# A four-layer transformer-like kernel on one core: every piece moved to a newly found place, six filler matmuls left out

## The chip, the cores and the metric

One Trainium2 chip, one NeuronCore, one launch. The time is device microseconds of one execution. The kernel before takes 2603.42 us, the median of three runs (2602.71 to 2609.87).

## The reference, cut to what matters

32 batches (`B`), 256 tokens, 256 features, 16 heads of 16. Four layers follow each other for every batch; batches don't touch.

```python
# L0: layer norm over the whole (S, D) of a batch, FiLM and a gate from t, W_in; the same again, W_out; residual
# L1: token layer norm with scale and shift from a timestep; attention with a 16x256x256 bias and a mask; FF (256 -> 1024 -> 256)
x = x + (ctx @ Wo + bo)
x = x + _gelu2(_ln(x) * g2 + beta2 @ W1 + b1) @ W2 + b2
# L2: stencil: gradients and second differences over (S, D), times dt, max(., 0)
# L3: causal attention, then FF with the exact gelu; gate against the input
return x + g * (x2 - x)
```

## The kernel before, in words

The kernel is one program for five engines with no loop on the chip: `build` writes out each engine's instructions in order. TensorE (PE) does matmuls and the turns (transposes by the identity), VectorE (DVE) the additions, the score-plus-bias reductions and half of the evacuations of turned scores, ScalarE (ACT) the exponentials, gelus and the other half, GpSimd (POOL) mask additions, reciprocal roots and several elementwise steps, and SyncE (SP) issues every DMA. A semaphore wait stands ahead of each piece that needs one; an engine never passes a piece that waits.

**What sets the order.** Time is counted in ticks. Batch b of layer 1 begins at tick 64 b and of layer 3 at 64 b + 160 (`begin`); its eight units (pairs of heads, called `_1[b.n]` and `_3[b.n]`) are four ticks apart. Each piece has a place, in ticks from that begin: in `P` for the middle batches, in `OWN` for batches 0, 1 and the last two (-2, -1), in `SPLIT` for units of layer 3. `place` looks it up. Each engine runs through all ticks, and within a tick through its pieces in the fixed order of its function. So a place says only where a piece stands in its engine's own order, nothing of when it runs.

**Pieces that the prediction names**, in the order of the work: `n1_stats`, `n1_sum`, `n1_center` (L969), `n1_scale` (L974, L978), `n1_gate` (L982), `win`, then the same with `n2_` (`n2_ones` is a matmul with ones between statistics and sum), `wout`, `x1` (L1077 and the token statistics), `x1_rstd` on POOL, `x1_norm` on ACT, `ada` (L603, L605) on POOL, `t1` (turn, L1514), `q1`, `k1`, `v1`. A unit is `stack` (nine DMAs), `score0/1` (L1538), `bias0/1` (L1010), `exp0/1` (L1249), `flip0/1` (L1548), `ev0` (L1254) and `ev1` (L1017), `pv` (L1563), `cx`, `ct`, `pvn`. Behind attention come `c1`, `o1`, `m1`, `t2`, `t2_out`, `t2_lo`, `w1` (four steps, L1447), `w1_out` (L1275), `w1_gelu`, `w2` (L1525), `f1`, the stencil `s_...` (`s_re` is L1122 and L1126), `m3`, `t3` and the same in layer 3: `c3` (turn), `c3_out`, `o3`, `m4`, `m4_norm`, `t4` (turn), `t4_out` (L1373), `t4_lo` (L949), `w3` (L1447), `w3_out`, `w3_gelu`, `w4` (L1525), `out`. `xb` (L595), `y3`, `q3_lo`, `k3_lo`, `mask_add` are POOL's. In the set-up, `film`, `adas` (L747), `split_p1` with `_hi` (`first_gains`, L834 to L854; `first_spread` on PE, L1470) and `_lo` (L860) make conditioning rows and scaled half-precision weights; `t1_lo` is L1085.

In each step of `w1` and `w3` the next step writes the one bank that ACT's `w1_out` or `w3_out` must first have read. Only for the last batch do two banks alternate.

**Fillers.** `warm` issues matmuls of the identity whose result nobody reads; `keep` does so behind a named piece of a named batch, by the table `WARM`, and waits for VectorE's last `pvn` first. One filler shows as two instructions (L1397) in the profile.

`Lane.wait_ge` drops a wait whose value its engine has already waited for.

Of the kernel before, what the change touches and what calls it, by code (L numbers as in the profile page):

```python
# [49 lines left out]
def begin(layer, b):  # L50
# [6 lines left out]
    "score0": -1, "score1": -1, "bias0": 0, "bias1": 0, "exp0": 1, "exp1": 2, "flip0": 8, "flip1": 8, "ev0": 7,  # L57
    "ev1": 9, "pv": 14, "cx": 13, "ct": 17, "pvn": 17, "ld_bt": -12, "mask_add": -23, "stack": -8, "ld_x": -78,
    "ld_xn": -37, "ld_ab": -36, "ld_mask": -117, "mask": -34, "n1_stats": -75, "n1_ones": -69, "n1_sum": -69,
# [6 lines left out]
    "f1": 74, "s_pm": 63, "s_b": 67, "s_r": 75, "s_rp": 82, "s_re": 96, "s_ha": 81, "s_w": 97, "s_ab": 97,  # L66
    "s_row": 98, "s_mm": 103, "s_f": 103, "ld_w1": -24, "ld_sten": -46, "ld_w3": -277, "coefs": -21,
# [6 lines left out]
    "out": 74, "st_out": 71,  # L74
# [32 lines left out]
        "y3": 60, "m4_rstd": 249, "m4_b": 298, "ld_x": -76, "ld_xn": -71, "ld_ab": -70, "ld_mask": -17,  # L107
        "ld_bt_1": -13, "stack_1": -12, "s_row": 96, "stack_3": -39, "st_out": 840,
    },
# [7 lines left out]
        "t2_lo": 70, "f1": 89, "s_r": 94, "s_rp": 94, "s_re": 94, "s_ab": 99, "s_f": 104, "m3": -54, "t3_lo": -37,  # L117
# [7 lines left out]
        "m4_b": 656, "ld_x": -88, "ld_xn": -61, "ld_ab": -39, "ld_mask": -139, "ld_bt_1": -22, "stack_1": -17,  # L125
        "stack_3": 217, "st_out": 980,
    },
# [71 lines left out]
def build(nc, A, OUT, scr, NB=32):  # L199
# [21 lines left out]
    with ExitStack() as ctx:  # L221
# [427 lines left out]
        def vector():  # L649
# [382 lines left out]
            def front(t):  # L1032
# [6 lines left out]
                for b in at(t, "n1_center"):  # L1039
                    V.wait_ge(p_wout, b)  # L1040
                    all_center(XT, sm1, v_n1)
# [798 lines left out]
```

## Time and profile before

| what | value |
|---|---|
| time, median of three runs | 2603.42 us |
| the profiled execution, first to last instruction | 2603.7 us |
| busy: PE, PE weight load, DVE, ACT, POOL | 2470.5, 2005.6, 2043.6, 2115.3, 1536.1 us |
| instructions | 57961 |
| DMA | 287.67 MB, 110 GB/s on average |

An engine's busy time is the union of its instructions' time. A matmul's end is modelled and overlaps the next one's start, so a busy PE isn't a PE at its peak. The weight-load row (PEld) is TensorE too: it loads the next matmul's weights while one runs, and an idle stretch of more than some 0.1 us there, with a named releaser, is where TensorE waited for data. Idle time of an engine that nobody waits for costs nothing. The granted clock is a share of TensorE's full clock.

### The profile page before, as it was taken

Reading aid. Unit: us, or ns where it says so; the run is one execution under the profiler, and the core shown is the slowest. Engines: PE = TensorE matmul, PEld = TensorE weight load, DVE = VectorE, ACT = ScalarE, POOL = GpSimd, SP = SyncE. Lnnn points to the kernel's source line nnn. Section 1 sums busy time; section 2 is a strip of 40 time slices with the busy share of each in tenths; the row PEclk is TensorE's granted clock in tenths of the full one; section 3 lists DMA queues with packets and bytes.
Section 4 is the critical chain, followed back from the end, with each engine's and each line's share of the span. In section 5 each row is a group of like instructions: output and inputs, shape, how many; then the busy total and the mean of one; then the engine's idle time right before and its main releaser. Section 6 shows DMA issues by size and latency. Waiting matters only on the chain.

```text
span 2603.7 us, 57961 instructions
## 1 busy us (share of the span) xinstructions
PE 2470.5 (95%) x19148; PEld 2005.6 (77%) x19148; DVE 2043.6 (78%) x7387; ACT 2115.3 (81%) x4694; POOL 1536.1 (59%) x1487
## 2 busy tenths in 40 slices
PE   6878999999999999999999999999999999999987
PEld 5666778778877877887887788778878877877776
DVE  6787878788888778888787888878888888878653
ACT  2466888888898888889888888988888888888875
POOL 2566666556666656666665656666556576655421
PEclk6899999999999999999999999999999999999999
DMA  5433443333344333334443333444433344433211
GB/s 205 120 119 105 121 127 113 111 106 106 107 122 126 112 110 108 107 105 122 126 115 108 108 107 106 122 127 115 114 110 100 105 121 125 123 105 96 75 29 33
DMA packets 178537, 287.67 MB, mean 110 GB/s; under 512 B 46080, under 2 KB 99328, under 8 KB 177984
## 3 DMA queue, kind: packets, MB, share of 16 engines
q1 hardware_dynamic: 178240, 283.97, 38.5%
q8 instruction: 155, 2.54, 0.4%
q14 instruction: 142, 1.16, 0.2%
HBM read 174.64 MB, written 8.45 MB: 70 GB/s over the span
## 4 chain that ended last, share of the span: by engine, by line
PE 69%; DVE 15%; SPq 4%; ACT 4%; issue 3%; POOL 2%; DMA 2%; DVEq 0%; POOLq 0%; ACTq 0%
PE bank L1525 17%; PE bank L1447 12%; PE bank L1548 10%; PE bank L1538 6%; PE bank L1563 6%; PE bank L1507 6%; DVE PB L1010 4%; PE bank L1514 3%; SPq L496 3%; PE bank L1459 3%; PE bank L1701 2%; DVE bank L969 2%; PE bank L1436 2%; SPq L492 1%; DMA Ks<-KU 1%
## 5 line engine op out<-in xcount | busy, mean ns | idle before, releaser
L1249 ACT ACTIVATE PB<-PB,mx 128x256 f32<-128x256 f32 (+1 forms) x2048 | 831.4, 473 | 35.7 <-DVE mx L1010 34.7
L579 POOL TENSOR_TENSOR BT<-BT,MN 128x1024 f32<-128x1024 f32 x256 | 556.9, 2180 | 122.5 <-DMA BT<-in_bias 121.0
L1548 PE MATMUL bank<-ident,PB 128*128 128x128 f32 x3584 | 486.4, 274 | 11.5 <-ACT PT L1254 5.5
L1010 DVE CUSTOM_DVE_ANT_0 PB<-bank,BT 128x256 f32<-128x256 f32 x1024 | 372.0, 418 | 137.8 <-PE bank L1538 132.8
L1548 PEld LDWEIGHTS bank<-ident,PB 128*128 128x128 f32 x3584 | 421.6, 141 | 63.4 <-ACT PB L1249 10.6
L1447 PE MATMUL bank<-TN,WS_w 128*128 128x256 f16 x3072 | 378.8, 273 | 38.7 <-ACT BB L1275 19.6
L1538 PE MATMUL bank<-Ks,Qs 96*128 96x512 f32 (+1 forms) x1024 | 364.6, 430 | 25.5 <-DMA Ks<-KU 12.0
L1017 DVE COPY PT<-bank 128x512 f32<-128x512 f32 (+1 forms) x512 | 315.9, 617 | 87.5 <-PE bank L1548 85.8
L1447 PEld LDWEIGHTS bank<-TN,WS_w 128*128 128x128 f16 x3072 | 282.5, 98 | 120.1 <-ACT BB L1275 35.4
L1254 ACT ACTIVATE PT<-bank 128x512 f32<-128x512 f32 (+1 forms) x512 | 272.3, 532 | 94.9 <-PE bank L1548 90.6
L1010 DVE CUSTOM_DVE_ANT_0 PB<-bank,caus 128x128 f32<-128x128 f32 (+1 forms) x1024 | 306.6, 350 | 42.3 <-PE bank L1538 42.2
L1563 PE MATMUL bank<-PT,VW 128*32 128x256 f32 (+1 forms) x4096 | 248.2, 360 | 4.4 <-DVE CX L1027 2.4
L1525 PE MATMUL bank<-Wf,BB 128*128 128x256 f32 x1024 | 236.8, 379 | 0.8 <-ACT BB L1264 0.6
L1525 PE MATMUL bank<-Wf,AA 128*128 128x256 f32 x1024 | 236.0, 383 | 0.5 <-ACT AA L1351 0.4
L1538 PEld LDWEIGHTS bank<-Ks,Qs 96*128 96x128 f32 x1024 | 168.1, 192 | 67.7 <-DVE mx L1010 22.3
L1525 PEld LDWEIGHTS bank<-Wf,AA 128*128 128x128 f32 x1024 | 192.2, 191 | 29.5 <-issue 0.9
L1525 PEld LDWEIGHTS bank<-Wf,BB 128*128 128x128 f32 x1024 | 189.6, 190 | 25.1 <-issue 1.7
L1563 PEld LDWEIGHTS bank<-PT,VW 128*32 128x32 f32 x4096 | 107.5, 109 | 98.7 <-issue 49.0
L554 POOL TENSOR_SCALAR smm<-smm 128x2 f32<-128x2 f32 x32 | 7.2, 226 | 280.0 <-DVE smm L991 280.0
L1010 DVE DVE_READ_ACCUMULATOR2_ANT mx<- 128x1 f32 x2048 | 169.0, 83 | 0.0
L1275 ACT ACTIVATE BB<-bank,cols 128x256 f32<-128x256 f32 x256 | 107.4, 470 | 44.3 <-PE bank L1447 44.3
L1260 ACT ACTIVATE ET<-bank 128x256 f32<-128x256 f32 x256 | 97.2, 380 | 46.8 <-PE bank L1563 42.7
(285 smaller groups left out, 4735.9 us busy)
## 6 DMA issues: line engine op xcount, KB each, us to landing
BT<-in_bias SPq DMA_DIRECT2D x256, 512.0 KB, 4.3
Qs<-QH SPq DMA_DIRECT2D x512, 64.0 KB, 2.4
Ks<-KH SPq DMA_DIRECT2D x1024, 32.0 KB, 2.0
Qs<-QU SPq DMA_DIRECT2D x256, 64.0 KB, 2.4
Ks<-KU SPq DMA_DIRECT2D x512, 32.0 KB, 2.0
XT<-in_xT SPq DMA_DIRECT2D x32, 256.0 KB, 2.8
X<-in_x SPq DMA_DIRECT2D x32, 256.0 KB, 2.9
AB<-ada_rows SPq DMA_DIRECT2D x32, 256.0 KB, 3.7
```

The costliest lines, as they stand in the source:

```text
L579: G.op.tensor_tensor(v2(BT[k % 4]), v2(BT[k % 4]), MN[:, :].unsqueeze(1).broadcast_to([128, 2, 512]), ALU.add).then_inc(g_bt, 1)
L1010: V.op.tensor_tensor_reduce(PB[(2 * D + q) % 6][:, h * 256:h * 256 + w], bS[q][:, h * w:h * w + w], plus, -1.0, 3.0e38, ALU.add, ALU.min, ...
L1017: V.op.tensor_copy(flipped(u.D, 1)[:, 0:w], bP[1][:, 0:w]).then_inc(v_ev, 1)
L1249: S.op.activation(o, o, ACT.Exp, scale=-1.0, bias=mx[u.layer][:, c:c + 1]).then_inc(a_exp, 1)
L1254: S.op.activation(flipped(u.D, 0)[:, 0:w], bP[0][:, 0:w], ACT.Copy).then_inc(a_ev, 1)
L1275: S.op.activation(half(out, m), half(ps, m), ACT.Identity, scale=scale(m), bias=bias(m)).then_inc(sem, 1)
L1447: last = T.op.matmul(half(ps, m), w, v[:, k * 256:k * 256 + 256], start=(k == 0 and i == 0), stop=(k == 1 and i == 2))
L1507: last = T.op.matmul(half(ps, m), x[:, k * 256 + m * 128:k * 256 + m * 128 + 128], Wf[:, a + k * 256:a + k * 256 + 256], start=(k == 0), s ...
L1525: last = T.op.matmul(half(ps, q), x[:, f * 256 + q * 128:f * 256 + q * 128 + 128], Wf[:, c:c + 256], start=(g == 0 and f == 0 and q == 0), ...
L1538: T.op.matmul(bS[q][:, 0:2 * w].rearrange("p (h k) -> p h k", h=2), Qs[i][0:96, et * 256 + q * 128:et * 256 + q * 128 + 128], k2[:, :, 0:w ...
L1548: last = T.op.transpose(bP[h][:, c * 128:c * 128 + 128], PB[(2 * u.D + q) % 6][:, h * 256 + k * 128:h * 256 + k * 128 + 128], ident[:, :])
L1563: last = T.op.matmul(half(bV, J % 2)[32 * s:32 * s + 32, q:256], VW[x][:, v:v + 32], flipped(u.D - 1 + et, h)[:, k * 256:k * 256 + 256 - q ...
```

## The change

All places of `P`, `OWN` and `SPLIT` are replaced by others, found by a search that replays the engines in order. No piece's instructions change. Six fillers go: one behind `n2_ones` of batch 2, four behind `n1_ones` of batch 3, one behind `v1` of batch 3. Two waits each are written ahead of `n1_center` and `n2_center`. The diff, cut to its core (the places of which the text speaks; the full tables change by a few ticks throughout):

```diff
 P = {
-    "cx": 13, "n1_stats": -75, "n1_sum": -69, "n1_gate": -53, "n2_center": -33, "x1": -29, "x1_norm": -27,
-    "n1_ones": -69, "v1_out": -7, "s_re": 96, "s_f": 103, "w2": 68, "m1": 49, "m1_rstd": 30, "m1_b": 56,
-    "t4": 58, "t4_out": 56, "y3": -8, "q3_lo": -37, "k3_lo": -33, "stack": -8, "st_out": 71,
+    "cx": 14, "n1_stats": -70, "n1_sum": -67, "n1_gate": -48, "n2_center": -36, "x1": -28, "x1_norm": -25,
+    "n1_ones": -68, "v1_out": -10, "s_re": 97, "s_f": 104, "w2": 69, "m1": 50, "m1_rstd": 24, "m1_b": 32,
+    "t4": 56, "t4_out": 55, "y3": -15, "q3_lo": -23, "k3_lo": -32, "stack": -6, "st_out": 83,
...
 WARM = {
-    "start": 24, "c1": 12, "n1_ones_0": 2, "v1": 9, "win_1": 5, "w1_0": 3, "n2_ones_2": 1, "n1_ones_3": 4,
-    "v1_3": 1, "v3": 10,
+    "start": 24, "c1": 12, "n1_ones_0": 2, "v1": 9, "win_1": 5, "w1_0": 3, "v3": 10,
 }
...
                 for b in at(t, "n1_center"):
                     V.wait_ge(p_wout, b)
+                    V.wait_ge(p_n1, b + 1)
+                    V.wait_ge(v_n1, 10 * b + 4)
                     all_center(XT, sm1, v_n1)
...
                 for b in at(t, "n2_center"):
                     V.wait_ge(p_win, b + 1)
+                    V.wait_ge(p_n2, b + 1)
+                    V.wait_ge(v_n2, 10 * b + 4)
                     all_center(FY, sm2, v_n2)
```

What this does to the engines' orders in a middle period of 64 ticks (brackets: batch, with +0 the one whose layer 1 begins there; all that isn't named keeps its order):

```text
PE    was: w2.2[-1], score[.2], w2.3[-1], flip[.0]       now: score[.2], w2.2[-1], flip[.0], w2.3[-1]
PE    was: flip_1[.4], pv_1[.3], t4[-3]                  now: flip_1[.4], t4[-3], pv_1[.3]
PE    was: score_3[-2.7], n1_ones[+2], w1.1, flip_3      now: score_3[-2.7], w1.1, flip_3, n1_ones[+2]
ACT   was: exp1_1[.5], m4_norm, ev0_1[.4], win_out, t4_out   now: m4_norm, exp1_1[.5], ev0_1[.4], t4_out, win_out
ACT   was: exp1_1[.7], w3_out.1                          now: w3_out.1, exp1_1[.7]
ACT   was: x1_norm, exp0_3[-2.1], exp1_3[-2.1]           now: exp0_3[-2.1], exp1_3[-2.1], x1_norm
DVE   was: n1_gate, s_r, bias_1[.3], v3_out, bias_1[.4]  now: s_r, bias_1[.3], v3_out, bias_1[.4], n1_gate
DVE   was: n2_sum, ev1_1[.5], pvn_1[.3], n2_center       now: n2_sum, n2_center, ev1_1[.5], pvn_1[.3]
DVE   was: bias0_3[-2.0], s_re, bias1_3[-2.0], ev1, n2_gate   now: bias0_3, bias1_3, ev1, n2_gate, s_re
DVE   was: x1, bias0_3[-2.1], bias1_3[-2.1]              now: bias0_3[-2.1], bias1_3[-2.1], x1
DVE   was: s_f, bias0_3[-2.2], bias1_3[-2.2]             now: bias0_3[-2.2], bias1_3[-2.2], s_f
POOL  was: q3_lo, k3_lo, mask_add[.6]                    now: mask_add[.6], k3_lo, mask_add[.7], m4_rstd, q3_lo
SP    was: st_out, stack_3[-2.6], ld_x, ld_bt[+1.0]      now: stack_3[-2.6], ld_bt[+1.0], st_out, ld_bt[+1.1], ld_x
```

In the set-up (batch 0) `split_p1_hi` moves on DVE from ahead of `n2_center` to behind `n2_gate` (on PE it stays ahead of `wout`), `x1` from behind `split_p1_lo` to ahead of it, and `adas` from behind `n1_gate` to ahead of it; on PE `win[1]` and `n2_ones[1]` come ahead of the first scores. At the end `w3` of batch 30 is spread between the scores of batch 31, and the last step of `w4[30]` moves from behind `t4[31]` to ahead of it.

## Rows read from the trace of the kernel before

**Rows 1.** The page, part 1: busy us (share of the span), instructions

```profile
PE 2470.5 (95%) x19148; PEld 2005.6 (77%) x19148; DVE 2043.6 (78%) x7387; ACT 2115.3 (81%) x4694; POOL 1536.1 (59%) x1487
```

**Rows 2.** Three stretches: PE, PEld, DVE, ACT, POOL busy, granted clock, DMA share, GB/s

```profile
0.00:300.00 300.00, 239.72 (x1588) 189.40 (x1589) 226.66 (x737) 162.89 (x346) 160.61 (x150) 0.86 0.45 139
300.00:2300.00 2000.00, 1962.76 (x15485) 1601.74 (x15484) 1631.07 (x5938) 1730.19 (x3851) 1252.38 (x1213) 1.00 0.40 112
2300.00:2604.00 304.00, 268.02 (x2079) 214.48 (x2077) 185.87 (x714) 222.18 (x498) 123.16 (x126) 0.99 0.26 69
```

**Rows 3.** The chain of waits, in order of time: start us, us, what

```profile
1193.77 5.29 PE bank L1525 x24
...
1269.21 5.29 PE bank L1525 x24
```

**Rows 4.** Waits of the weight loads, 1421 to 2025 us: us in total, times, longest

```profile
PEld bank L1447 <- ACT BB L1275: 8.7, 16, 0.7
...
PEld bank L1447 <- DVE TN L949: 4.3, 16, 0.3
...
PEld bank L1538 <- DVE mx L1010: 2.2, 8, 0.3
```

**Rows 5.** Timeline of the weight loads, one quiet period [idle before <-releaser]

```profile
1208.49 0.42 PEld L1514 LDWEIGHTS bank<-ident,CX 128*128 128x128 f32 x4 [0.17 <-issue]
...
1219.70 1.21 PEld L1447 LDWEIGHTS bank<-TN,WS_w 128*128 128x128 f16 x12 [0.31 <-DVE TN L949]
...
1228.77 0.19 PEld L1538 LDWEIGHTS bank<-Ks,Qs 96*128 96x128 f32 x1 [0.28 <-DVE mx L1010]
```

**Rows 6.** Timeline of ACT, the same period

```profile
1217.29 0.82 ACT L1275 ACTIVATE XT<-bank,cols 128x256 f32<-128x256 f32 x2
1218.33 0.60 ACT L1373 ACTIVATE TN<-bank 128x512 f16<-128x512 f32 x1 [0.22 <-PE bank L1514]
```

**Rows 7.** Timeline of DVE, the same period

```profile
1218.96 0.69 DVE L949 TENSOR_TENSOR TN<-bank,TN 128x512 f16<-128x512 f32 x1 [0.73 <-ACT TN L1373]
...
1223.49 1.77 DVE L969 SCALAR_TENSOR_TENSOR bank<-XT,sm,gT 128x512 f32<-128x512 f32 x1
...
1227.48 0.35 DVE L1122 TENSOR_TENSOR sme<-X,er 128x8 f32<-128x8 f32 x2
...
1227.95 0.41 DVE L1010 CUSTOM_DVE_ANT_0 PB<-bank,caus 128x256 f32<-128x256 f32 x1
...
1232.30 0.67 DVE L1077 TENSOR_TENSOR X<-bank,X 128x512 f32<-128x512 f32 x1
```

**Rows 8.** Timeline of POOL, the same period

```profile
1223.41 1.29 POOL L595 TENSOR_TENSOR X<-X,rows 128x512 f32<-128x512 f32 x1
...
1238.43 1.27 POOL L605 TENSOR_TENSOR X<-X,AB 128x512 f32<-128x512 f32 x1
```

**Rows 9.** Timeline of PE, the same period

```profile
1241.66 0.60 PE L1514 MATMUL bank<-ident,X 128*128 128x128 f32 x4
```

**Rows 10.** Timeline of PE, 100 to 420 us: fillers (L1397)

```profile
169.45 0.49 PE L1397 MATMUL bank<-ones,ident 128*128 128x128 f32 x2 [1.38 <-DVE CX L1027]
...
202.64 1.14 PE L1397 MATMUL bank<-ones,ident 128*128 128x128 f32 x8
```

**Rows 11.** One stretch behind the fillers, columns as rows 2

```profile
230.00:250.00 20.00, 15.84 (x102) 10.87 (x101) 19.61 (x69) 9.03 (x22) 11.32 (x13) 0.83 0.29 72
```

**Rows 12.** Timeline of DVE, set-up of batch 0

```profile
29.88 0.67 DVE L747 TENSOR_TENSOR PB<-bank,PB 32x512 f32<-32x512 f32 x1
...
36.01 0.27 DVE L834 TENSOR_REDUCE ap<-bank 4x1 f32<-4x128 f32 x1
...
39.45 0.75 DVE L969 SCALAR_TENSOR_TENSOR bank<-XT,sm,gT 128x512 f32<-128x512 f32 x1
...
56.42 0.75 DVE L1085 SCALAR_TENSOR_TENSOR H<-bank,wp,H 128x512 f16<-128x512 f32 x1 [3.12 <-ACT H L1330]
```

**Rows 13.** Timeline of PE, the last 30 us

```profile
2586.02 1.89 PE L1525 MATMUL bank<-Wf,BB 128*128 128x256 f32 x8
```

More of the change, by code:

```diff
@@ L56 @@
 P = {
-    "score0": -1, "score1": -1, "bias0": 0, "bias1": 0, "exp0": 1, "exp1": 2, "flip0": 8, "flip1": 8, "ev0": 7,
-    "ev1": 9, "pv": 14, "cx": 13, "ct": 17, "pvn": 17, "ld_bt": -12, "mask_add": -23, "stack": -8, "ld_x": -78,
-    "ld_xn": -37, "ld_ab": -36, "ld_mask": -117, "mask": -34, "n1_stats": -75, "n1_ones": -69, "n1_sum": -69,
[6 rows of a table removed]
-    "f1": 74, "s_pm": 63, "s_b": 67, "s_r": 75, "s_rp": 82, "s_re": 96, "s_ha": 81, "s_w": 97, "s_ab": 97,
-    "s_row": 98, "s_mm": 103, "s_f": 103, "ld_w1": -24, "ld_sten": -46, "ld_w3": -277, "coefs": -21,
+    "score0": -1, "score1": -1, "bias0": 0, "bias1": 0, "exp0": 2, "exp1": 3, "flip0": 8, "flip1": 8, "ev0": 7,
+    "ev1": 9, "pv": 14, "cx": 14, "ct": 17, "pvn": 17, "ld_bt": -13, "mask_add": -26, "stack": -6, "ld_x": -71,
+    "ld_xn": -41, "ld_ab": -37, "ld_mask": -85, "mask": -31, "n1_stats": -70, "n1_ones": -68, "n1_sum": -67,
[6 rows of a table added]
+    "f1": 73, "s_pm": 59, "s_b": 60, "s_r": 74, "s_rp": 81, "s_re": 97, "s_ha": 74, "s_w": 98, "s_ab": 98,
+    "s_row": 101, "s_mm": 103, "s_f": 104, "ld_w1": -24, "ld_sten": -46, "ld_w3": -277, "coefs": -21,
     "split_p1": -55, "split_p1_hi": -50, "split_p1_lo": -45, "split_w1": -8, "split_w1_hi": -4, "split_w1_lo": -2,
     "split_p3": 46, "split_p3_hi": 50, "split_p3_lo": 54, "split_w3": 82, "split_w3_hi": 88, "split_w3_lo": 92,
[4 rows of a table removed]
-    "out": 74, "st_out": 71,
[4 rows of a table added]
+    "st_out": 83,
 }
@@ L91 @@
     -2: {
[15 rows of a table removed]
-        "y3": 60, "m4_rstd": 249, "m4_b": 298, "ld_x": -76, "ld_xn": -71, "ld_ab": -70, "ld_mask": -17,
-        "ld_bt_1": -13, "stack_1": -12, "s_row": 96, "stack_3": -39, "st_out": 840,
[6 rows of a table added]
+        "m1": 50, "t2_lo": 60, "f1": 80, "s_r": 82, "s_rp": 90, "s_re": 91, "s_ab": 99, "s_f": 112, "m3": -46,
[9 rows of a table added]
     },
     -1: {
[6 rows of a table removed]
-        "t2_lo": 70, "f1": 89, "s_r": 94, "s_rp": 94, "s_re": 94, "s_ab": 99, "s_f": 104, "m3": -54, "t3_lo": -37,
[7 rows of a table removed]
-        "m4_b": 656, "ld_x": -88, "ld_xn": -61, "ld_ab": -39, "ld_mask": -139, "ld_bt_1": -22, "stack_1": -17,
-        "stack_3": 217, "st_out": 980,
-    },
[10 rows of a table removed]
-        "s_rp": 86, "s_re": 97, "s_w": 99, "s_ab": 102, "s_f": 109, "t3_lo": -44, "bias1_3": 0, "v3_out": 15,
[8 rows of a table removed]
-        "s_row": 93, "stack_3": -10, "st_out": 84,
-    },
[7 rows of a table removed]
-        "t2_lo": 62, "f1": 84, "s_r": 85, "s_rp": 92, "s_re": 92, "s_w": 98, "s_ab": 98, "s_f": 102, "m3": -38,
[7 rows of a table removed]
-        "ld_mask": -32, "ld_ab": -21, "ld_bt_1": 0, "stack_1": 4, "s_row": 100, "stack_3": -8, "st_out": 75,
[6 rows of a table added]
+        "t2_lo": 70, "f1": 86, "s_r": 90, "s_rp": 93, "s_re": 97, "s_ab": 98, "s_f": 101, "m3": -54, "t3_lo": -39,
[7 rows of a table added]
+        "m4_b": 734, "ld_x": -100, "ld_xn": -68, "ld_ab": -27, "ld_mask": -100, "ld_bt_1": -14, "stack_1": -12,
+        "stack_3": 273, "st_out": 1017,
+    },
[17 rows of a table added]
+        "y3": -33, "m4_rstd": 33, "m4_b": 55, "scr": -390, "ld_mask": -325, "ld_sten": -150, "ld_ab": -181,
+        "ld_w1": -71, "ld_w3": -93, "ld_bt_1": 0, "stack_1": 0, "s_row": 103, "stack_3": -13, "st_out": 89,
+    },
[7 rows of a table added]
+        "t2_lo": 63, "f1": 80, "s_r": 80, "s_rp": 85, "s_re": 94, "s_w": 97, "s_ab": 97, "s_f": 101, "m3": -50,
[7 rows of a table added]
+        "ld_mask": -31, "ld_ab": -41, "ld_bt_1": -8, "stack_1": -1, "s_row": 91, "stack_3": -13, "st_out": 75,
     },
@@ L168 @@
 SPLIT = {
-    "bias1_3": 1, "exp0_3": 2, "exp1_3": 3, "ev0_3": 8, "ev1_3": 10, "pv_3": 13, "cx_3": 12, "ct_3": 16,
-    "pvn_3": 18, "stack_3": -9,
+    "bias1_3": 0, "exp0_3": 2, "exp1_3": 3, "ev0_3": 8, "ev1_3": 10, "pv_3": 13, "cx_3": 13, "ct_3": 17, "pvn_3": 18,
+    "stack_3": -7,
 }
```

135 rows, old and new, of tables (OWN, P) are left out of this document.

## The prediction, made before the changed kernel was built or run

> **What bounds the kernel now.** I read the page's busy times first: TensorE is busy for 95% of the span, the next engine for 81% [rows 1]. Then the stretches: TensorE's idle time is 60 us in the first 300 us, 37 us in the 2000 us of the middle and 36 us in the last 304 us [rows 2], and its granted clock is full from 300 us on. So the middle is a TensorE stream that another order can't make shorter than its own issue time, and what is to be gained there are short waits that recur in each batch.
>
> The chain of waits gives the period: the same block of 24 matmuls comes at 1193.77 and at 1269.21 us, 75.44 us apart [rows 3]. 28 such periods lie between some 200 and 2300 us; the rest is filling and draining. A busy matmul row hides small waits behind its modelled end, so I go to the weight loads, where they show as idle time with a releaser. Over eight periods (1421 to 2025 us) the largest is L1447 waiting for ScalarE's L1275, 8.7 us for layer 3 alone, 1.09 us a period [rows 4]: the steps of `w3` share one bank with `w3_out`. Smaller are L1447 waiting for VectorE's L949 (`t2_lo`, `t4_lo`), 4.3 us, and L1538 waiting for L1010 (a score that waits for the reductions of the unit before), 2.2 us in 8 times, so once in every period [rows 4]. Places of the kind last named in the table of orders are what the change can mend.
>
> **The change part by part.**
>
> *The added waits* cost nothing. `n1_sum` and `n2_sum` stand ahead of their `center` in both orders and have waited for the same values, so `Lane.wait_ge` issues no instruction. Instructions are the same but for 12 (six fillers), DMAs the same and in number and size.
>
> *`t4` and `t4_out` earlier.* Now `t4_out` starts at 1218.33 behind `win_out` of 0.82 us [rows 6], `t4_lo` at 1218.96 after 0.73 us of idle VectorE [rows 7], and the first `w3` step's weights at 1219.70 after 0.31 us idle, released by it [rows 5]. With `m4_norm` ahead of two exponentials, `t4` ahead of `pv` (some 1 us) and `t4_out` ahead of `win_out`, that input comes at least 0.6 us earlier, and the wait of 0.31 us goes whole. Between 0 and 0.31; I take 0.31. What is late next is the bank's hand-over between the steps of `w3`, whose filling work on PE is the same as before: that 1.09 us stays.
>
> *`s_re` behind `bias1_3[-2.0]`.* From 1227.48 to 1227.95 VectorE does the two edge products and sums between two reductions [rows 7]; the score behind waits 0.28 us for the second reduction [rows 5]. Moved behind, the reduction ends 0.47 us sooner and the wait is gone: 0.28. `s_re` itself feeds the DMA `s_row`, for which `s_mm` has not to wait here; that cover is the three `w4` and score blocks ahead of it.
>
> *`n1_gate` behind `v3_out`.* An elementwise step of 0.67 to 0.69 us [rows 7] leaves the way of `v3_out`, for which `c3` waits (its wait names no releaser, the two are 0.2 us apart): 0.17 [rows 5]. `n1_gate` feeds `win`, two units later on PE; nobody is behind it.
>
> *Given back.* `x1` goes behind four reductions (0.3 to 0.4 us each, 1.4 together, by the one of 0.41 [rows 7]). It starts the longest side chain: `x1` at 1232.30 [rows 7], roots, `x1_norm`, the last `ada` step at 1238.43 for 1.27 us [rows 8], the turn `t1` at 1241.66 [rows 9]. Between the end of `ada` (1239.70) and `t1` there are 1.96 us. Of these 1.4 go, and 0.76 because TensorE comes earlier: 0.2 short; with ScalarE's `x1_norm` also behind four exponentials I take 0.3 us, between 0 and 1.68 (the whole of a further 1.48 us of exponentials, less nothing). `w3_out.1` ahead of `exp1`, `n1_ones` behind two turns, `v1_out` and `ev1` earlier, the spacing of `w2`: each moves a piece into or out of a stretch of at most 0.2 us; together 0, between -0.2 and +0.2. On POOL `q3_lo`, `k3_lo` both go behind `mask_add[.6]`, which no longer waits for ScalarE; `stack_3[-2.0]` needs them 10 ticks later: 0. On SP the stacks are held by their buffers, the same two scores ahead as before, so the new places of `st_out` and `ld_mask` change nothing: 0. `m1_b` now stands ahead of masks and waits for `m1_norm`; behind it on POOL are `m3_rstd` and the mask additions of the next batch, four units early: 0.
>
> So a period gives 0.31 + 0.28 + 0.17 - 0.30 = 0.46 us, 28 periods 12.9 us.
>
> *Fillers.* Eight filler instructions take 0.89 us start to start (202.64 to the next block at 203.53; the row's 1.14 has the modelled end) [rows 10], so twelve take 1.3 us. The filler of batch 2 also waited 1.38 us for a `pvn` [rows 10]. Both lie where TensorE idles anyway, so between 0 and 2.7 us; I take 1.5.
>
> *Set-up.* `first_gains` runs on VectorE from 36.01 to 39.45, right ahead of `n2_center` [rows 12]; moved behind `n2_gate` it gives that chain 3.4 us, and takes back some 1 us as `first_spread` on PE stays ahead of `wout`. `adas` ahead of `n1_gate` can't begin before TensorE's rows are there, at 29.88 [rows 12], and holds the gate for 1.5 us. Net 0.9 us by `x1`. But `split_p1_lo` then follows `x1`: some 4 us of VectorE work in front of `t1_lo`, which had 3.12 us of idle time ahead of it [rows 12]. So nothing is left of it at batch 0. The front of batch 1 (`win`, `n2_ones` ahead of the first scores) gets earlier by a few us, into a stretch where TensorE idles 20%. I take 1.0 us for all, between -3 and +6.
>
> *End.* The `w3` steps of batch 30 between scores of batch 31 fill waits of about 1 us each, some 2.5 us; the last `w4` step ahead of `t4[31]` puts up to 1.89 - 0.4 us in the way of the last chain [rows 13]. I take 1.0, between -2 and +4.
>
> Sum: 12.9 + 1.5 + 1.0 + 1.0 = 16.4 us off the profiled execution's 2603.7, which is 2587.3. That execution stands 0.3 us above the median of the runs, so 2587.
>
> **A rule against the trace.** `n2_center` takes 1.77 us [rows 7] where the same instruction takes 0.75 us in the set-up [rows 12]; POOL's `xb` runs from 1223.41 to 1224.70 [rows 8] beside the long one, and nothing on POOL beside the short. The change puts `n2_center` ahead of `ev1` and `pvn`, so ahead of `xb`, which waits for `n2_rstd` in POOL's order. Then 1.0 us leaves a stretch in which VectorE has no idle time from 1218.96 to 1228.6. This is the rival "larger" below. The Trainium skill ("SBUF — State Buffer", "Summary: rules for kernel authors") says that a VectorE instruction with two SBUF inputs and a GpSimd instruction that reads SBUF block each other, the second waiting for the first to end. By that rule the trace agrees: 1.77 is 0.75 plus 1.02 us.
>
> **The rivals.**
>
> *Larger:* the stretch of VectorE leads TensorE, and the 1.0 us comes on top of 0.46. At most the rest of what weight loads lose there: 28 x 1.0 would be 28; I count half, 14 us: 2573. Against: the named waits for VectorE in the middle are 0.31 + 0.28 us only.
>
> *Given back:* the period is set by the hand-over of the banks and by stacks that land just in time, and the waits mended come back one block later. 0.1 us a period, 2.8, with 3.5 for the rest: 2597.
>
> *Slower:* the chain from `x1` to `t1` comes late. 1.4 us on VectorE and 1.48 us on ScalarE, less the 1.96 of slack, are 0.92 us; `t1` then opens 0.92 us later than now in each period and drags all with it: 25.8 us, less 3.5: 2626. It decides from a delay of 1.96 us on; at 2.3 us the kernel is slower by over 0.3%. For: two engines put the chain behind others. Against: the exponentials can run before `x1_norm`'s roots are ready.
>
> *Clock:* without the fillers the granted clock falls once more. Behind them a stretch of 20 us already has 0.83 [rows 11], which is an alternation of 1.2 and 2.4 GHz; 20 us at 0.83 lose 3.4 us, where TensorE waits anyway. That gives 2590. The Trainium skill ("TensorE: Matmul & The Clock Gate", "Why this matters for your kernels") says that an idle gap drops the clock by half; by it twelve short instructions between others decide nothing, and no run here shows it yet.
>
> *No difference by design:* the waits that are written and not issued are the part of the change that does nothing; a search whose replay misjudges waits could as well end at 2603. It is in "given back".
>
> **How the numbers follow.** Forecast (2579 to 2595) 0.46, clock 0.04 beside it; larger 0.14; given back (2595 to 2609) 0.26; slower 0.10. 0.3% is 7.8 us, about what a measurement of this kernel can tell from no change: faster lies below 2595.6, slower above 2611.2. Faster 0.46 + 0.03 + 0.14 = 0.63, slower 0.10, same 0.27. The range leaves out the slower rival and the far side of the larger one: 2571 to 2608; the forecast's own is 2579 to 2595.
>
> **What would show it.** Right: a period near 75.0 us; no L949 wait ahead of the first `w3` step; no L1010 wait at the score behind `w3.3`; `c3` without its 0.17; L969 of `n2` near 0.8 us. The slower rival: L1514 `<-X` waits for POOL L605 in each period. Given back: same period, other releasers. Wrong altogether: if the gain lies in the first 300 or the last 300 us, or if stacks' DMAs show as the new wait of L1538.

## The result, and the profile after

The changed kernel takes 2638.13 us, the median of four runs (2636.57 to 2643.31), against 2603.07 us of the kernel before on the same chip: a ratio of 1.0134, 95% interval 1.0116 to 1.0151. It is slower by 35 us, and I had forecast 16 us faster. The profiled execution takes 2637.3 us. Times below come from several sessions, in which the kernel before had medians of 2603.1 to 2608.6 us, so runs are compared by their ratio to it.

The page's busy times after answer to [rows 1]. The stretches, in the columns of [rows 2], stand behind them.

```profile
PE 2468.8 (94%) x19136; PEld 2005.4 (76%) x19136; DVE 1991.6 (76%) x7387; ACT 2110.4 (80%) x4694; POOL 1539.3 (58%) x1487
```

```profile
0.00:300.00 300.00, 232.27 (x1500) 181.48 (x1501) 205.34 (x712) 156.97 (x332) 155.10 (x144) 0.85 0.43 135
300.00:2300.00 2000.00, 1938.66 (x15391) 1585.60 (x15389) 1586.68 (x5890) 1710.38 (x3819) 1251.71 (x1205) 1.00 0.40 112
2300.00:2640.00 340.00, 297.91 (x2250) 238.35 (x2248) 199.54 (x788) 243.06 (x544) 132.51 (x140) 0.96 0.25 66
```

TensorE's work is the same and its idle time in the middle has grown from 37 to 61 us, at a full clock. VectorE is busy 52 us less: its instructions are the same, so some of them got shorter, and TensorE got nothing of it.

The place of the loss shows when the same piece is compared in both traces. The first matmul of `win` of each batch starts, against the kernel before, in the profiled executions:

| kernel | batch 2 | batch 4 | batch 29 | end | a period, batches 4 to 29 |
|---|---|---|---|---|---|
| before | 160.41 us | 302.62 us | 2197.91 us | 2603.7 us | 75.81 us |
| changed | -0.2 | +8.5 | +24.0 | +33.6 | 76.43 us |

So 8.5 us are lost while the pipeline fills, 15.5 us over 25 middle periods (0.62 each, where I had forecast a gain of 0.46) and 9.6 us behind batch 29.

Each row is one execution, and the ends scatter from one execution to the next. The kernel before, run 10 and run 11 below have the same instructions in the same order up to `win` of batch 2, and it starts at 160.4, 154.1 and 157.7 us; runs 2 and 12 are the same up to `win` of batch 4, and it starts at 310.8 and 314.2 us. So a difference of under some 6 us at batch 2, or 3 us at batch 4, shows nothing by itself.

The waits of the middle answer to [rows 4]. From the waits of the changed kernel, 1421 to 2025 us (engine, line, releaser: us in total, times, longest):

```profile
PEld bank L1539 <- DMA Ks<-KU: 11.1, 15, 1.3
PEld bank L1448 <- ACT BB L1276: 9.7, 16, 0.8
...
PE bank L1539 <- DMA Ks<-KU: 7.3, 13, 1.1
...
PEld bank L1539 <- issue: 6.6, 16, 0.4
...
PEld bank L1448 <- DVE TN L946: 1.9, 8, 0.2
```

The two waits that I wanted mended are: the one for TN went from 4.3 us in 16 times to 1.9 in 8 (only layer 1's is left), the one for `mx` in 8 times is off the list. In their place scores wait for the stacks, 15 times in eight periods, so twice in each. The same in the whole kernel, first a row of the page of before and then two of the changed kernel's page (busy us, mean ns, idle before and its releaser):

```profile
L1538 PE MATMUL bank<-Ks,Qs 96*128 96x512 f32 (+1 forms) x1024 | 364.6, 430 | 25.5 <-DMA Ks<-KU 12.0
```

```profile
L1539 PE MATMUL bank<-Ks,Qs 96*128 96x512 f32 (+1 forms) x1024 | 362.5, 431 | 60.9 <-DMA Ks<-KU 53.3
...
L1539 PEld LDWEIGHTS bank<-Ks,Qs 96*128 96x128 f32 x1024 | 167.9, 193 | 119.3 <-DMA Ks<-KU 70.3
```

What is behind such a wait stands in the chain of waits of the changed kernel (start us, us, what):

```profile
1421.67 0.64 ACT KH L1293
1422.38 0.96 POOL KU L564
1423.63 1.28 POOL QU L561
1424.93 0.57 SPq L489
...
1430.05 2.40 DMA Ks<-KU
1432.49 0.73 PE bank L1539 x2
...
1459.29 0.72 POOL smt L554
1460.28 1.25 POOL QU L561
1461.54 0.56 SPq L489
...
1467.41 2.01 DMA Ks<-KU
1469.46 0.62 PE bank L1539 x2
```

Two chains in one period, both through POOL and SP. In the first, `k1_lo` (KU) waits for ScalarE's `k1_out`, `q1_lo` (QU) runs behind it, and only then can SP issue the nine DMAs of `stack_1[+1.0]`, the first three of which carry Q. In the second, `q3_lo` stands in POOL's order behind `mask_add[.7]` and `m4_rstd` (smt); `stack_3[-2.0]` begins at 1461.54 us, where `q3_lo` has just ended (1460.28 + 1.25). POOL's order in a middle period has changed by more than the table of orders says. The two places that matter, in both kernels:

```text
was: m1_rstd, q1_lo, k1_lo, mask_add[.0], m3_rstd            now: m1_rstd, k1_lo, q1_lo, m1_b, mask, m3_rstd, mask_add[.0]
was: mask_add[.4], q3_lo, mask_add[.5], s_pm, k3_lo,         now: mask_add[.4], mask_add[.5], s_pm, s_b, mask_add[.6],
     mask_add[.6], s_b, mask_add[.7], m4_rstd                     k3_lo, mask_add[.7], m4_rstd, q3_lo
```

The same stretch in POOL's and SP's timelines, and the row of POOL's waits over eight periods:

```profile
1456.39 2.14 POOL L576 TENSOR_TENSOR BT<-BT,MN 128x1024 f32<-128x1024 f32 x1
1458.71 0.23 POOL L551 TENSOR_SCALAR smt<-smt 128x2 f32<-128x2 f32 x1 [0.18 <-DVE smt L988]
...
1460.23 1.29 POOL L561 TENSOR_TENSOR QU<-QU,QH 128x512 fp32r<-128x512 f32 x1
```

```profile
1457.22 0.58 SPq L465 DMA_DIRECT2D X<-in_x  x1
1461.54 0.56 SPq L489 DMA_DIRECT2D Qs<-QH  x1
```

```profile
POOL smt L551 <- DVE smt L988: 5.1, 8, 0.9
```

SP is free at 1457.80 us, and the last score that reads the stack's buffer has started at 1456.97; SP then stands still for 3.7 us until `q3_lo` is done. `m4_rstd` waits for VectorE's statistics, but only 0.18 us here and 0.2 to 0.9 us in the eight periods. The rest is POOL's own work: the end of the mask addition (0.7 us), the four steps of `m4_rstd` (1.6) and `q3_lo` itself (1.3). The kernel before has `q3_lo` long before it is wanted. Its POOL, SP and PE timelines, in the period of [rows 5]:

```profile
1199.20 1.28 POOL L564 TENSOR_TENSOR QU<-QU,QH 128x512 fp32r<-128x512 f32 x1 [0.27 <-ACT QH L1292]
...
1214.47 0.71 POOL L557 TENSOR_TENSOR smt<-smt,mh 128x2 f32<-128x2 f32 x1
```

```profile
1213.26 0.56 SPq L492 DMA_DIRECT2D Qs<-QH  x1
1213.86 0.59 SPq L492 DMA_DIRECT2D Qs<-QU  x1
1214.49 0.59 SPq L492 DMA_DIRECT2D Qs<-QH  x1
1215.12 2.57 SPq L496 DMA_DIRECT2D Ks<-KH  x4
1217.73 1.23 SPq L496 DMA_DIRECT2D Ks<-KU  x2
```

```profile
1223.37 0.60 PE L1538 MATMUL bank<-Ks,Qs 96*128 96x256 f32 x2
```

`q3_lo` is done 12.8 us before the first DMA of `stack_3[-2.0]`, the stack's nine DMAs keep SP for 5.7 us, and its first score starts at 1223.37 us, 10.1 us behind the stack's start and without waiting for it. In the changed kernel the stack starts 7.9 us before its first score, which waits for it. The stack is late by what `q3_lo` is late, and `q3_lo` is late because it stands seven pieces further back. No run puts `q3_lo` between `k3_lo` and `m4_rstd`, so what each of the seven costs isn't shown.

### The profile page after: what moved, and what is told of

The parts are those of the page before. It is cut to its first block, busy times and chain, and to the rows that moved or that the text cites. A ratio compares the mean times of both kernels' runs of the same rounds, so it can differ in the third digit from the quotient of the medians.

```text
span 2637.3 us, 57930 instructions
## 1 busy us (share of the span) xinstructions
PE 2468.8 (94%) x19136; PEld 2005.4 (76%) x19136; DVE 1991.6 (76%) x7387; ACT 2110.4 (80%) x4694; POOL 1539.3 (58%) x1487
## 4 chain that ended last, share of the span: by engine, by line
PE 66%; SPq 12%; POOL 6%; DMA 5%; DVE 5%; ACT 4%; issue 2%; POOLq 0%; DVEq 0%; ACTq 0%
PE bank L1526 17%; PE bank L1448 13%; PE bank L1549 9%; SPq L493 7%; PE bank L1564 6%; PE bank L1508 6%; PE bank L1539 6%; DMA Ks<-KU 4%; SPq L489 4%; POOL QU L561 2%; PE bank L1515 2%; PE bank L1702 2%; PE bank L1460 2%; ACT PB L1250 1%; PE bank L1574 1%
## 5 line engine op out<-in xcount | busy, mean ns | idle before, releaser
L1250 ACT ACTIVATE PB<-PB,mx 128x256 f32<-128x256 f32 (+1 forms) x2048 | 841.2, 474 | 46.7 <-DVE mx L1007 45.7
L1276 ACT ACTIVATE AA<-bank,cols 128x256 f32<-128x256 f32 x256 | 107.4, 471 | 42.6 <-PE bank L1448 42.3
```

What stands on the lines that cost most here:

```text
L1250: S.op.activation(o, o, ACT.Exp, scale=-1.0, bias=mx[u.layer][:, c:c + 1]).then_inc(a_exp, 1)
L1276: S.op.activation(half(out, m), half(ps, m), ACT.Identity, scale=scale(m), bias=bias(m)).then_inc(sem, 1)
```

## The experiments

**Theory A:** POOL's low halves (`q_lo`, `k_lo`) come late in POOL's order, the stacks start late, the scores wait. **Rival B:** the chain from `x1` to `t1` comes late, as in the prediction's slower rival, and the stacks only slip along.

**1. Low halves back, in both layers.**

```diff
 P = {   (the changed kernel's, middle batches)
-    "q1_lo": -33, "k1_lo": -38, "q3_lo": -23, "k3_lo": -32
+    "q1_lo": -27, "k1_lo": -27, "q3_lo": -37, "k3_lo": -33
```

> The changed kernel with q1_lo, k1_lo, q3_lo and k3_lo of the middle batches back where they stood on POOL; every other engine's order is the changed kernel's. Theory A (POOL's low halves come late behind m1_rstd, the mask additions and m4_rstd, the stacks' DMAs behind them, the scores wait for Ks): in 1421 to 2025 us the changed kernel's weight loads at L1539 wait 11.1 us for Ks where the kernel before has 1.2. That 10 us over eight periods is 1.2 us a period, and the period was 0.85 us longer; A expects that wait at 1 to 3 us, a period of 75.0 to 75.6 us and a time of 2612 to 2624 us, since filling and draining, with 17 of the 35 us lost, stay as they are. Rival B (the chain from x1 to t1 comes late, my rival of the prediction, and the stacks wait only because the whole period slipped): the period stays at 76.2 to 76.6 us and the time at 2633 to 2640 us, the wait for Ks turning into a wait of L1515 for X.

Measured: 2819.12 us, ratio 1.0815 (1.0793 to 1.0837). Neither theory: the places, taken from the old table, don't give the old order. `m1_b`, `mask` and `m3_rstd` have moved ahead in the new one, so that `q1_lo` and `k1_lo` came to stand behind all three.

**2. and 3. One layer at a time.** Layer 3 alone (in POOL's order only `q3_lo` moves, back ahead of `s_b`, `mask_add[.6]`, `k3_lo`, `mask_add[.7]` and `m4_rstd`), and layer 1 alone with the unlucky place.

```diff
-    "q3_lo": -23, "k3_lo": -32      (2)
+    "q3_lo": -37, "k3_lo": -33
-    "q1_lo": -33, "k1_lo": -38      (3)
+    "q1_lo": -27, "k1_lo": -27
```

> The changed kernel with only layer 3's q3_lo and k3_lo put back. Theory A expects that the one late stack_3[-2.0] goes and the one late stack_1[+1.0] stays: half of the gain of putting all four back, 7 to 11 us, so 2626 to 2632 us. A variant of A in which only one of the two decides (A3: q3_lo, which goes from 37 to 23 ticks ahead and behind m4_rstd, the longer move): all of the gain, 2612 to 2624 us. Rival B (x1 to t1): 2633 to 2640 us.

> The changed kernel with only layer 1's q1_lo put back ahead of k1_lo. Theory A with equal shares: 2626 to 2632 us. A3 (layer 3 alone decides): 2634 to 2640 us. Rival B: 2633 to 2640 us. If this run gives the whole gain and the one with layer 3 none, the swap of q1_lo and k1_lo, which I had not even costed, is the cause.

Measured: layer 3 alone 2617.88 us, ratio 1.0046 (1.0030 to 1.0061); layer 1 alone 2846.89 us, ratio 1.0924. One instruction of 1.28 us in an earlier place gives back 0.88% of 1.34%, some 23 us: rival B is out as the main cause. In the profiled executions it gives back 17.3 us between batches 4 and 29, 0.69 a period. Run 3 is no test of layer 1, but a price: behind `m1_b`, `mask` and `m3_rstd` instead of ahead of them, the two halves of layer 1 make a period 83.7 us long (mean over batches 4 to 29). From `m1_rstd`'s end at 1460.10 us to `q1_lo`'s start at 1466.24 us run 3 has 1.68 us in which `m1_b` waits for ScalarE and 4.5 us of POOL's own work. That wait, 1421 to 2025 us:

```profile
POOL X L614 <- ACT AA L1270: 11.7, 7, 1.7
```

With layer 3 mended (run 2), the same stretch still shows one late stack in each period:

```profile
PEld bank L1539 <- DMA Ks<-KU: 4.2, 8, 1.2
```

**4. The cause alone.** The kernel before with POOL's new order of the four pieces: `q3_lo` behind `m4_rstd`, `q1_lo` behind `k1_lo`.

```diff
 P = {   (the kernel before)
-    "q1_lo": -27, "k1_lo": -27, "q3_lo": -37, "k3_lo": -33
+    "q1_lo": -26, "k1_lo": -27, "q3_lo": -23, "k3_lo": -32
```

> The kernel before with only POOL's order of q1_lo, k1_lo, q3_lo and k3_lo of the middle batches as in the changed kernel. Theory A: the cause alone, without anything else of the change, makes the kernel before slower by 0.5 to 0.85 us a period over 28 periods: 2617 to 2627 us, and its weight loads at L1538 wait for Ks some 8 to 11 us between 1421 and 2025 us, where they wait 1.2 us now. Rival B: 2600 to 2606 us, no difference. Between them (2607 to 2615): the move costs only together with others that use up the stacks' slack.

Measured: 2638.82 us, ratio 1.0126 (1.0104 to 1.0148). These places alone make the kernel before as slow as the whole change does, but not in the same stretches: from batch 4 to 29 it loses 25.8 us, 1.03 a period, where the change loses 15.5. That the totals agree is chance; that these places bring the wait for Ks and a loss of this size is shown. The waits of the weight loads and of the matmuls, 1421 to 2025 us:

```profile
PEld bank L1538 <- DMA Ks<-KU: 13.5, 16, 2.2
...
PE bank L1538 <- DMA Ks<-KU: 9.4, 14, 2.0
```

**5. Layer 1 put right.** As run 2, with `q1_lo` directly ahead of `k1_lo`.

```diff
-    "q1_lo": -33      (run 2)
+    "q1_lo": -39
```

> The changed kernel with q3_lo and k3_lo of layer 3 back (which alone gave 2618 us) and q1_lo of layer 1 back ahead of k1_lo, where ada's last instruction and m1_rstd stand ahead of both as before. Behind the scores at L1539 the run with layer 3 alone still waits 4.2 us in 8 times for Ks between 1421 and 2025 us, once a period, 0.5 us each. Theory A (every late low half costs): that wait goes, 0.3 to 0.5 us a period over 28 periods, so 2604 to 2610 us. Rival (the swap is covered, only layer 3's halves count): 2615 to 2620 us.

Measured: 2609.67 us, ratio 1.0018 (1.0006 to 1.0030). The swap costs 0.28%, 7 us (0.41%, 11 us, if run 12 is set against run 2), and its wait is gone:

```profile
PEld bank L1539 <- DMA Ks<-KU: 0.8, 3, 0.3
```

From batch 4 to 29 this kernel gains 11.1 us on the kernel before, 0.44 a period, near what the forecast gave for the middle. Run 7, and runs 13 and 15 below, which have this order from batch 4 on, gain 0.41, 0.34 and 0.38. But it comes 15.5 us late to batch 4 and loses 5.4 us behind batch 29.

**6. and 7. Old tables for the ends.** As run 5, with the old tables of the first two and last two batches and all fillers (6), or the old tables of the last two alone (7).

```diff
-OWN = { ... }    (new)
+OWN = { ... }    (of before: 0, 1, -2, -1 in run 6; -2, -1 in run 7)
```

> As the run with all low halves back, and the tables of the first two and the last two batches and the fillers as in the kernel before; the middle batches keep the changed places. Theory A (the rest of the loss is filling and draining, 8 us in batches 2 and 3 and some 9 us behind the last input matmuls): 14 to 18 us less than that run, and 8 to 13 us faster than the kernel before if my three mended waits (0.46 us a period) are worth what I put them at: 2591 to 2597 us. Rival C (given back: the mended waits come back as others): 2601 to 2606 us. If the loss of the first 300 us stays, it comes from the middle places reaching into batches 2 and 3, not from the set-up's tables.

> As the run with all low halves back, and only the tables of the last two batches as in the kernel before. Against the run with all low halves back it gives the price of draining: theory A 7 to 10 us less; a rival, that the end only drags along what came late before, 0 to 3 us less.

Measured: 2664.18 us, ratio 1.0209 (1.0183 to 1.0236), and 2649.18 us, ratio 1.0164 (1.0148 to 1.0181). Both missed: old ends on a new middle are worse than new ends. Run 6 is 22.1 us late at batch 4, run 7 loses 39 us behind batch 29. The tables of the ends fit only the middle that they were found with, so these runs don't give a price of the ends.

**8. The three mended waits alone, on the kernel before.**

```diff
-    "m4_norm": 54, "t4": 58, "t4_out": 56, "win_out": -41, "s_re": 96, "n1_gate": -53
+    "m4_norm": 53, "t4": 56, "t4_out": 55, "win_out": -40, "s_re": 97, "n1_gate": -48
```

> The kernel before with only the three moves for which I forecast the gain: m4_norm, t4 and t4_out earlier, s_re behind bias1_3[-2.0], n1_gate behind v3_out. Without the delayed x1 chain my terms are 0.31 + 0.28 + 0.17 = 0.76 us a period, 21 us over 28: 2582 us if each is worth its wait. Rival C (a mended wait comes back at the next hand-over, since the period is set elsewhere): 2598 to 2606 us. In the trace the wait of L1447 for TN before the first w3 step (4.3 us over eight periods with both layers) and that of L1538 for mx (2.2 us) should be gone in either case.

Measured: 2598.78 us, ratio 0.9976 (0.9965 to 0.9988): 0.24% faster than the kernel before, with run 9 the lowest ratio here. From batch 4 to 29 it gains 10.7 us, 0.43 a period (0.31 and 0.35 in runs 14 and 16 below, which have the same three moves), where the three terms make 0.76. The waits of 1421 to 2025 us show where the rest may have gone:

```profile
PEld bank L1447 <- ACT BB L1275: 9.7, 16, 0.8
PEld bank L1447 <- ACT AA L1275: 7.6, 21, 0.5
PEld bank L1538 <- issue: 6.6, 16, 0.4
...
PEld bank L1447 <- DVE TN L949: 1.6, 7, 0.2
```

TN's wait fell by 2.7 us and that for `mx` (2.2) is gone. But the hand-over of the bank between the `w3` steps rose by 1.0 us against [rows 4], and the score's wait without a releaser from 3.3 us in 8 times (a row of the kernel before) to 6.6 in 16. So 4.3 of the 4.9 us mended came back as other waits. The period gained 3.4 us in eight, more than the difference; wait rows are no full account of a period, and least of all can their sums be taken as a gain.

**9. `n2_center` ahead of `ev1` and `pvn`, on top of run 8.**

```diff
-    "n2_center": -33
+    "n2_center": -36
```

> The kernel before with the three mended waits and also n2_center ahead of ev1_1[.5] and pvn_1[.3], as the change has it. My rival larger: n2_center's 1.7 us fall towards 0.75 because POOL's xb no longer runs beside it, 1 us a period on VectorE, 14 us of the time at half the worth: 2585 us. Its other face, as the periods of 75.07 us with the three mends alone suggest: VectorE isn't what TensorE waits for, L969 gets shorter and the time stays within 3 us of the run with the three mends, 2596 to 2602 us.

Measured: 2602.84 us, ratio 0.9975 (0.9963 to 0.9987), the same as run 8. Durations of that line, `n1_center` and `n2_center` together, 1421 to 2025 us, in the kernel before and in this run (min/median/max ns):

```profile
L969 DVE SCALAR_TENSOR_TENSOR bank<-XT,sm,gT x16: 751/1760/2006, 1450.7 to 2022.2; 128x512 f32<-128x512 f32 x16
```

```profile
L969 DVE SCALAR_TENSOR_TENSOR bank<-XT,sm,gT x16: 748/952/2028, 1446.8 to 2018.1; 128x512 f32<-128x512 f32 x16
```

The eight of `n2_center` alone are the clearer reading: 1.76 to 1.77 us each in the kernel before, 0.75 us each in this run (0.75 in the changed kernel too). So the instruction does get 1.0 us shorter when POOL's `xb` isn't beside it, and the time stays.

**10. `x1` late, alone.**

```diff
-    "x1": -29, "x1_norm": -27
+    "x1": -27, "x1_norm": -25
```

> The kernel before with x1 alone behind four reductions, ev1_1[.7] and pvn_1[.5] (1.1 us of reductions from 1233.90 to 1234.98 us and some 1.3 us for the two others, more than in the change) and x1_norm behind exp0_3[-2.1] and exp1_3[-2.1]. My rival slower: 2.4 us on VectorE are 0.4 us over the slack of 1.96 us, and ScalarE's exponentials can add up to 1.48: the turn t1 comes 0.4 to 1.9 us late in each period, 11 to 53 us more, 2614 us or above, L1514 waiting for X of L605. The other theory, after the period of 75.1 us that the changed kernel reaches once POOL's low halves are back: the chain has more slack than I read, and the time stays at 2602 to 2609 us.

Measured: 2620.00 us, ratio 1.0048 (1.0029 to 1.0067). The forecast of the time was near; its mechanism was not. From batch 4 to 29 the run loses 1.2 us, 0.05 a period, so a delay of some 2.4 us on VectorE (the estimate of its expectation) fits into the slack. At batch 4 it is 7.2 us behind. (At batch 2 it is 6.3 us ahead, but its instructions are still those of the kernel before there, so that is scatter.) Between the two `x1` stands behind `pvn_1[.5]`, and that piece waits for the stencil's DMA through TensorE. From its chain of waits:

```profile
247.41 1.72 DMA AA<-AA
...
249.26 1.97 PE bank L1701 x8
251.23 0.23 PE bank L1573 x2
251.48 0.22 DVE rd L1024
...
251.93 0.69 DVE X L1077
```

The kernel before has `x1` at 247.17 us. In the change `x1` is behind reductions only.

**11. Without the six fillers, alone.**

```diff
-    "w1_0": 3, "n2_ones_2": 1, "n1_ones_3": 4, "v1_3": 1, "v3": 10
+    "w1_0": 3, "v3": 10
```

> The kernel before without the six fillers, nothing else. My term: 0 to 2.7 us less, 1.5 taken: 2602 us. The rival clock: TensorE's granted clock falls more often between 140 and 240 us, 3 to 5 us more: 2607 to 2609 us, with a granted clock below 0.91 in stretches where it is 0.91 to 1.00 now.

Measured: 2605.08 us, ratio 0.9988 (0.9979 to 0.9997), 3 us less. The granted clock looks lower. From the stretches of 20 us of the kernel before and of this run:

```profile
160.00:180.00 20.00, 15.14 (x118) 11.82 (x119) 17.89 (x64) 11.44 (x27) 13.36 (x11) 1.00 0.20 59
180.00:200.00 20.00, 16.25 (x124) 12.12 (x124) 14.53 (x34) 10.36 (x20) 10.19 (x15) 0.91 0.24 78
```

```profile
160.00:180.00 20.00, 14.93 (x103) 11.99 (x96) 17.39 (x61) 10.29 (x25) 11.71 (x12) 0.86 0.09 22
180.00:200.00 20.00, 18.07 (x122) 14.28 (x123) 12.46 (x27) 9.54 (x19) 8.99 (x12) 0.80 0.24 77
```

But it scatters as much with all six fillers there: in the same two stretches run 10 has 0.81 and 0.76, run 8 has 0.91 and 0.83, run 6 has 0.95 and 0.67. So no run shows that the fillers hold the clock.

**12. `q1_lo` back from batch 4 on only.** Run 5, with `q1_lo` of batches 2 and 3 as in the change.

```diff
+    2: {"q1_lo": -33}, 3: {"q1_lo": -33}      (in OWN)
```

> The changed kernel with q3_lo back everywhere and q1_lo back only from batch 4 on (batches 2 and 3 keep it behind k1_lo, as the search found it). The run with both back everywhere lost 7 us more than this order in batches 1 to 3 (15.5 us behind the kernel before at batch 4, where the changed kernel is 8.5 behind) and gained 11 us from there to batch 29. If the place in batches 2 and 3 makes those 7 us: 2601 to 2604 us, no difference from the kernel before, and 8 us behind at batch 4. If they come from q3_lo or from elsewhere: 2608 to 2612 us.

Measured: 2611.41 us, ratio 1.0005 (0.9993 to 1.0018): no difference from the kernel before. Against the kernel before it is 11.5 us behind at batch 4, 0.3 ahead at batch 29 (a gain of 0.47 a period) and 4.8 behind at the end.

**13. `x1` earlier in batches 2 and 3, on top of run 12.**

```diff
+    2: {"x1": -30, "x1_norm": -28}, 3: {"x1": -30, "x1_norm": -28}      (in OWN)
```

> The run with q3_lo back and q1_lo back from batch 4 on (11.5 us behind the kernel before at batch 4), now also with x1 and x1_norm of batches 2 and 3 earlier, ahead of the reductions and exponentials that the change put in front of them. The kernel before with x1 alone late lost 6.5 us at exactly this place and nothing behind it. Theory D (the places in P reach into the filling, where x1 to t1 has no slack): 4 to 7 us of the 11.5 come back, 2601 to 2605 us with the kernel before at about 2605. Rival E (the loss there is made by the late statistics of m1 and by k1_lo ahead of q1_lo, in the chain at 197 to 209 us): 0 to 2 us, 2606 to 2612 us.

Measured: 2613.65 us, ratio 1.0030 (1.0016 to 1.0044), 11.6 us behind at batch 4. The place of `x1` isn't what the filling loses; moved forward it gives nothing back.

**14. Runs 8 and 11 together.**

```diff
-    "m4_norm": 54, "t4": 58, "t4_out": 56, ...      (all of run 8)
+    "m4_norm": 53, "t4": 56, "t4_out": 55, ...
-    "n2_ones_2": 1, "n1_ones_3": 4, "v1_3": 1      (run 11)
```

> The kernel before with the three mended waits and without the six fillers. If the two parts (ratios 0.9976 and 0.9988 alone) add: 0.9964, some 9 us less than the kernel before. If the fillers' gain was chance or the falling clock costs as much as they do: 0.9976, some 6 us less.

Measured: 2604.36 us, ratio 0.9983 (0.9970 to 0.9995). The parts don't add.

**15. and 16. Fillers again.** Run 12 with five of the six back (15), and run 8 with only the one at `n2_ones` dropped (16).

```diff
+    "n1_ones_3": 4, "v1_3": 1      (15, to run 12)
-    "n2_ones_2": 1                 (16, from run 8)
```

> The run with q3_lo back and q1_lo back from batch 4 on, and five of the six fillers back: four behind n1_ones and one behind v1 of batch 3. In both kernels that had the order of before in the filling, taking the fillers out lost some 5 us between the input matmuls of batches 2 and 4, at a granted clock of 0.80 to 0.86 where it had been 0.91 to 1.00. Theory F (the missing fillers make that part of the filling's loss): 3 to 5 us less than the same order without them, so at or just below the kernel before, ratio 0.998 to 0.9995, and the loss at batch 4 falls from 11.5 to 6 to 8 us. Rival G (the fillers do nothing for the time, as in the whole kernel's time with the order of before): ratio 1.000 to 1.003, loss at batch 4 unchanged.

> The kernel before with the three mended waits and only the one filler dropped that waited 1.38 us for a pvn (behind n2_ones of batch 2). Theory F: the five others keep the clock, and the loss of 5 us between batches 2 and 4 of the run without any of the six is gone: ratio 0.9965 to 0.9976 against the kernel before, 6 to 9 us less. Rival G: as without all six, 0.998.

Measured: ratios 1.0001 (0.9988 to 1.0014) and 0.9980 (0.9966 to 0.9994); run 15 is 12.3 us behind at batch 4. Rival G stands: five fillers more or less can't be told apart in the time. Between 180 and 200 us run 15 has them and shows

```profile
180.00:200.00 20.00, 18.46 (x118) 15.09 (x118) 13.71 (x41) 9.29 (x20) 7.35 (x6) 0.74 0.21 70
```

## Why the prediction was wrong

**The step that failed** is one sentence: "On POOL `q3_lo`, `k3_lo` both go behind `mask_add[.6]`, which no longer waits for ScalarE; `stack_3[-2.0]` needs them 10 ticks later: 0." I took a distance in ticks for a time and named no row of POOL (and by the tables the distance of `q3_lo` is 16 ticks, not 10). In ticks `q3_lo` was early enough; on the engine it now stood behind seven more pieces, the last of them `m4_rstd`, and was done 3.7 us after SP had become free for the stack. Put at 0, it measured 0.88% or 23 us (the change against run 2). The swap of `q1_lo` and `k1_lo` stood in neither my list of orders nor my sum and measured 0.28% to 0.41% or 7 to 11 us (run 2 against runs 5 and 12). With `q3_lo` undone everywhere and the swap from batch 4 on the ratio falls from 1.0134 to 1.0005 (run 12), and both on the kernel before make 1.0126 of it (run 4). The sentence that SP's new places change nothing was blind to what SP waits for; no run tries SP's places alone. The prediction did name the sign, the stacks' DMAs as the new wait of L1538, and gave it no chance.

**The sum of the middle** came out near the forecast once POOL was right: 0.34 to 0.47 us a period (runs 5, 7, 12, 13 and 15) for 0.46. That is luck, two errors that cancel. The three mended waits were put at 0.76 and are worth 0.31 to 0.43 (runs 8, 14 and 16); the waits for the hand-over of the bank and at the next score grew meanwhile. That was my rival "given back", true for about half. The delayed chain from `x1` was put at -0.30 and costs 0.05 even where it is delayed by more (run 10).

**Filling** was put at +1.0 and the fillers at +1.5. The change loses 8.5 us by batch 4. The fillers' term is right within its bounds (3 us in run 11, nothing in run 15). A loss is there: the six kernels with the new order in batches 0 to 3 and `q3_lo` right are 8.2 to 15.5 us behind at batch 4 (runs 2, 5, 7, 12, 13, 15), five with the old order are -1.2 to 2.9 us behind (runs 8, 9, 11, 14, 16). What makes it isn't settled: not `x1`'s place (run 13), not the fillers (run 15), and not `q1_lo`'s, for which the place that the search found is no worse there (15.5 and 13.6 us in runs 5 and 7, 11.5 to 12.3 in runs 12, 13 and 15, 8.2 in run 2). In the changed kernel `m3_rstd` of batch 0 gets its statistics on POOL at 196.74 us, 4.5 us later than before (192.21), and `k1_lo`, `q1_lo` and the stack of batch 2 stand behind it (the expectation of run 13 took that piece for `m1`'s). What makes the statistics late I haven't isolated.

**The end** was put at +1.0, and the change loses 9.6 us behind batch 29. That this comes from the new tables of the last two batches isn't shown: with the old tables the same stretch is 2.9 us longer in run 10, 4.1 in run 8, 5.5 in run 9, 8.0 in run 14, 9.4 in run 16 and 11.2 in run 4, and 1.2 us shorter in run 11, always against the one execution of the kernel before. The new order of `w3` and `w4` at the end wasn't tried alone.

**The rivals.** *Larger* is out: `n2_center` got shorter and the time didn't (run 9). The rule of the Trainium skill ("SBUF — State Buffer", "Summary: rules for kernel authors") agrees with the length of `n2_center`, which falls from 1.76 to 0.75 us away from POOL's reads; it says nothing of who waits. *Slower through `x1`* is out for the middle (run 10) and in the filling of the change (run 13). *Clock* isn't borne out: without the fillers the time is 3 us less and not 3 us more (run 11), and the granted clock of those stretches scatters between executions with all six fillers as well, so that they make it fall isn't shown.

## What to carry to other kernels

A piece ends no sooner than all that stands ahead of it in its engine's order, the work and the waits; so for a moved piece add up what each piece now in front of it takes and waits for, and look at who is released by it, in the timeline and not in the plan's ticks. Check the small, cheap pieces on the engine with the most idle time (POOL, 58% busy) as carefully as the big ones: a 1.3 us instruction five pieces later in the order, in each period, cost 23 us. Mending named waits brought about half of them here, in a stream that is bound by one engine, and tables of the ends found together with a middle were worse with another one. Before a few us of a trace's ends are explained, look at two executions that have the same instructions up to there.

## What the runs showed of the hardware

Two things I had not expected. Between 160 and 200 us, where TensorE is busy for 14 to 18 of 20 us, the granted clock of a stretch of 20 us lies anywhere between 0.67 (run 6, which has all fillers) and 1.00 from one run to the next (below 1.00 an alternation of 1.2 and 2.4 GHz), with the fillers or without, and fillers more or less went with 3 us of the time at most. And a queue on SP is slow enough to be a term of its own: nine DMAs of one stack, issued one after the other, take at least 5.7 us of SP's time (0.6 each) and their data lands 2.0 to 2.4 us behind the start of the last, so a piece that releases a stack has to be done some 8 us before the score.
